# A gated delta-rule layer with expert mixing: a new body of the pass, with masked scaled decays, 32x32 turns and solves in two steps

## What is computed

```python
def step(state, inp):
    q_t, k_t, v_t, g_t, b_t = inp
    state = state * jnp.exp(g_t)[..., None, None]
    kv_mem = jnp.einsum('bhkv,bhk->bhv', state, k_t)
    delta = (v_t - kv_mem) * b_t[..., None]
    state = state + jnp.einsum('bhk,bhv->bhkv', k_t, delta)
    o = jnp.einsum('bhkv,bhk->bhv', state, q_t)
    return (state, o)
```

## Time and profile before

| | us |
|---|---|
| median of three runs | 3445.3 (3440.46 to 3448.35) |
| the profiled execution | 3440.67 |
| its span, first to last instruction | 3438.8 |
| zc of the first pass to zc of the last, 63 passes | 337.2 to 3388.5 |
| mean granted TensorE clock | 0.953 |

### The profile page before, as it was taken

One profiled execution on the slowest core, in us unless ns is written; L12 is line 12 of the kernel. 1 busy time (PEld: TensorE's weight loads), 2 busy tenths in 40 slices (PEclk: granted clock), 3 DMA queues, 4 the chain that ended last, 5 costly groups with the idle time before them and its releaser, 6 DMA issues.

```text
span 3438.8 us, 56504 instructions
## 1 busy us (share of the span) xinstructions
PE 2992.4 (87%) x18444; PEld 2451.1 (71%) x18444; DVE 3012.3 (88%) x9101; ACT 1794.2 (52%) x4111; POOL 2306.0 (67%) x2650
## 2 busy tenths in 40 slices
PE   7844999989998989899989988898989899998997
PEld 4422777778776777677767777777777777777776
DVE  5996999989998999899989898998899898989996
ACT  3322555555554555455545555555555555555553
POOL 0005777777767776777778777877777667877764
PEclk9976999999999999999999999999999999999999
DMA  1003545544555545454545554544555454544553
GB/s 60 1 1 104 137 132 141 135 131 132 137 139 135 131 133 139 130 133 133 141 126 138 134 138 124 149 127 134 138 138 137 125 139 132 146 129 135 144 132 89
DMA packets 541827, 427.98 MB, mean 124 GB/s; under 512 B 247008, under 2 KB 450784, under 8 KB 541536
## 3 DMA queue, kind: packets, MB, share of 16 engines
q1 hardware_dynamic: 476000, 222.98, 24.0%
q0 software_dynamic: 65536, 201.39, 22.0%
HBM read 345.61 MB, written 45.09 MB: 114 GB/s over the span
## 4 chain that ended last, share of the span: by engine, by line
DVE 36%; POOL 35%; PE 14%; issue 9%; DMA 5%; ACT 1%; SPq 0%; DVEq 0%; POOLq 0%; ACTq 0%
POOL rows L952 22%; DVE rows L1193 9%; POOL xg L931 9%; DVE qkv L1177 6%; DVE mix L1210 4%; POOL rms L928 3%; DVE E L1165 3%; DMA rows<-table,pick 3%; PE ps L579 3%; PE ps L500 3%; PE ps L517 2%; PE ps L665 1%; DVE topi L1024 1%; DVE xg L1147 1%; PE ps L521 1%
## 5 line engine op out<-in xcount | busy, mean ns | idle before, releaser
L952 POOL DMA_INDIRECT rows<-table,pick x1024 | 1157.2, 1130 | 326.3 <-issue 326.3
L551 PE MATMUL ps<-X,AT 128*128 128x128 f32 x3072 | 417.7, 294 | 119.2 <-DMA XT<-whole 119.2
L551 PEld LDWEIGHTS ps<-X,AT 128*128 128x128 f32 x3072 | 392.9, 207 | 169.8 <-DMA XT<-whole 167.3
L806 ACT ACTIVATE qkv<-qkv 128x512 f32<-128x512 f32 x256 | 161.5, 631 | 518.6 <-DVE qkv L1177 518.6
L571 PE MATMUL ps<-XT,E 128*128 128x128 f32 x3072 | 400.6, 277 | 0.0
L801 ACT ACTIVATE raw<-ps 128x512 f32<-128x512 f32 x256 | 152.8, 597 | 433.2 <-PE ps L517 433.2
L1210 DVE SCALAR_TENSOR_TENSOR mix<-rows,zc,mix 128x256 f32<-128x256 f32 x896 | 375.1, 476 | 0.0
L571 PEld LDWEIGHTS ps<-XT,E 128*128 128x128 f32 x3072 | 368.9, 192 | 0.0
L939 POOL TENSOR_SCALAR gm<-cst,gn 128x128 f32<-128x128 f32 x512 | 362.9, 723 | 6.7
L1193 DVE CUSTOM_DVE_ANT_0 rows<-rows,h2c 128x128 f32<-128x128 f32 x1024 | 342.9, 399 | 9.2 <-SPq L328 4.7
L931 POOL TENSOR_SCALAR xg<-xg,rms 128x128 f32<-128x128 f32 x520 | 324.9, 637 | 7.0
(11 more groups left out here) (167 smaller groups left out, 6333.4 us busy)
## 6 DMA issues: line engine op xcount, KB each, us to landing
Wvz<-wvz SPq DMA_DIRECT2D x64, 512.0 KB, 3.3
xb<-xnT SPq DMA_DIRECT2D x64, 512.0 KB, 4.4
whole<-AT SPq DMA_DIRECT2D x128, 256.0 KB, 3.6
X<-whole SPq DMA_DIRECT2D x128, 256.0 KB, 3.9
XT<-whole SPq DMA_DIRECT2D x128, 256.0 KB, 4.4
wo<-woh SPq DMA_DIRECT2D x65, 256.0 KB, 4.4
Wkq<-wkq SPq DMA_DIRECT2D x64, 256.0 KB, 2.5
rows<-table,pick POOLq DMA_INDIRECT x1024
```

The source lines that it names most:

```text
L551: done = mm(ps[:, g, (a % 4) * P:(a % 4 + 1) * P], AT_b[:, a, :], src[:, a, :], start=True, stop=True)
L952: pool.indirect_dma_start(rows[:, m, :], None, table[:, :], bass.IndirectOffsetOnAxis(ap=pick[:, m:m + 1], axis=0)).then_inc(gathered, 16)
```

## The change

The same 64 passes and pipelining, with a new body:

- **Masks and decays.** GpSimd makes gm with two `affine_select` (causal, 128x512 each) in place of eight products, and two more selects mask the decays DT after the exponential. ScalarE then scales the decays by head, in place (`scale_decays`, eight operations). With that, AT comes from two VectorE operations, straight from the key products in PSUM, with a factor of -1 and no identity; the elimination adds where it subtracted. MT comes from two VectorE operations, also straight from PSUM. km and kq, and GpSimd's MT products, are gone.
- **Levels.** Two in place of three. The first E is put with `copy_predicated` into E0, which holds the identity. XT comes from TensorE as before, and X from VectorE turning XT's PSUM in blocks of 32x32 (`turn_X`). The second E leaves PSUM as four small rectangles on ScalarE (`take_E`), into E1, which also holds the identity.
- **Solves.** The last level isn't formed. Each solve is done in two steps: XT times RV (`blocks`), ScalarE copies the upper half to Y, TensorE carries it to the lower half (`carried`), VectorE adds it to RV (`lower_rhs`), XT times RV again, ScalarE copies Y. `scaled_y` is gone, and Kd is scaled by kcol.
- **Second output.** Its product with MT moves from the end of the pass to the beginning of the next (`second_output`).
- **Order.** GpSimd's `finish` stands ahead of the picks, so that the sixteen gathers follow each other; the first eight wait for half_v (four mixes of each half done). VectorE's masked E stands ahead of the second outputs; mean_square comes behind key_norms and the fourth mix. On ScalarE squares and the RV copies stand ahead of silu(0).
- xb, a copy of the tokens' columns that SyncE loaded every pass, is gone; the projection reads xnT.

The diff, cut to its core:

```diff
@@ GpSimd @@
+            def causal(dst, src, done):
+
+                pool.affine_select(dst, src, [[0, 4], [1, P]], ALU.is_ge, zero, base=0, channel_multiplier=-1).then_inc(done, 1)
...
-                for a in range(TASKS):
-                    pool.tensor_scalar(gm[:, a, :], mask(C_LE), gn[:, a:a + 1], None, ALU.mult).then_inc(sm["gm_p"], 1)
+                for g in range(2):
+                    causal(gm[:, 4 * g:4 * g + 4, :], gn[:, 4 * g:4 * g + 4].unsqueeze(2).broadcast_to([P, 4, P]), sm["gm_p"])
...
-                pool.wait_ge(sm["diff_t"], at("diff_t", 2))
+                for g in range(2):
+                    pool.wait_ge(sm["exp_done"], at("exp_done", g + 1))
+                    d = DT[:, 4 * g:4 * g + 4, :]
+                    causal(d, d, sm["causal_p"])
                 if f + 1 < PASSES:
                     gate_sums(f + 1, 2 if n is None else 1)
                 if n is not None:
-                    pool.wait_ge(sm["e_v"], at("e_v", 3))
+                    finish()
+                    pool.wait_ge(sm["half_v"], at("half_v", 1))
                 picks(f)
...
                 gather(0)
                 if n is not None:
-                    finish()
                     pool.wait_ge(sm["mix_v"], at("mix_v", 1))
                 gather(K // 2)
...
-                    pool.tensor_tensor(MT2[nx][:, 4 * g:4 * g + 4, :].rearrange("p (t r) i -> p t r i", r=R),
...
@@ TensorE @@
                 if place["u"]:
+                    second_output(MT2[nx])
                     pe.wait_ge(sm["inv_in"], last("inv_in"))
...
+                    for g in range(2):
+                        pe.wait_ge(sm["e_v"], at("e_v", g + 1))
+                        if g == 0:
+                            pe.wait_ge(sm["o1_v"], at("o1_v", 1))
+                        elif place["u"]:
+                            pe.wait_ge(sm["qs_s"], last("qs_s"))
+                        level_X(0, g)
...
@@ ScalarE @@
                 if front:
                     take(0)
                 if back:
-                    take_X(0, 0)
                     take_XT(0, 0)
-                    take_X(0, 1)
-                if front:
-                    silu(0)
-                if back:
                     take_XT(0, 1)
                     act.wait_ge(sm["xg_v"], at("xg_v", 2))
                     squares(1)
...
+                if front:
+                    silu(0)
+                if back:
+                    take_E(0)
+                    take_E(1)
+                if front:
+                    act.wait_ge(sm["s_v"], at("s_v", 1))
+                    act.wait_ge(sm["causal_p"], at("causal_p", 2))
+                    scale_decays(0)
...
@@ VectorE @@
+                def turn_X(g):
+
+                    dve.wait_ge(sm["xt_t"], at("xt_t", g + 1))
+                    V.transpose(X[:, 4 * g:4 * g + 4, :].rearrange("p a i -> p (a i)"), ps[:, 4 + g, :]).then_inc(sm["x_v"], 1)
...
+                def triangle(r):
+
+                    dve.wait_ge(sm["scaled_s"], at("scaled_s", 4 * r + 4))
+                    V.scalar_tensor_tensor(out=of_head(AT, r), in0=keys_by_time(), scalar=-1.0, in1=of_head(DT, r), op0=ALU.mult, op1=ALU.mult)\
+                        .then_inc(sm["at_v"], 1)
...
-                    level(0, 0)
-                    level(0, 1)
                     dve.wait_ge(sm["silu_e"], at("silu_e", 1))
-                    expert_mix(0, 3)
+                    expert_mix(0, 1)
+                    turn_X(0)
+                    turn_X(1)
                 if front:
                     for d in (1, 2, 3):
                         tap(0, d)
                 if back:
+                    expert_mix(1, 3)
+                if front:
+                    key_norms()
+                if back:
                     expert_mix(3, 4)
-                    level(1, 0)
-                    level(1, 1)
-                if front:
-                    strict_part()
-                if back:
                     mean_square()
                 if front:
+                    triangle(0)
+                    triangle(1)
```

375 lines of the change are left out of this document (189 added, 186 removed).

## The result

The changed kernel takes 3771.1 us (median; 3759.6 to 3778.0) beside 3446.8 of the kernel before on the same chip: 1.094 times, 95% interval 1.090 to 1.097. It is slower, as forecast, but by 324 us where 205 were forecast, and outside the range of 3460 to 3740. The profiled execution took 3778.0 us, its span 3776.3.

The account below looks back on a forecast made before the run. Bound: a loop of GpSimd's gathers and scaling in series with VectorE's head and dots. 3.1 + 3.56 + 12.64 + 30.2 = 49.5 us, plus 1.6 for the clock; 3440.7 + 63 x 3.6 - 20 = 3647, say 3650; range 3460 to 3740.

Parts of the forecast that it names:

- VectorE's head, 12.64 + 1.6 for the clock = 14.2: From zc to mean_square landing, which GpSimd's rms awaits: 12.64 us, plus 1.6 for XT products at half clock.
- The rival in which the clock stays up: TensorE's clock doesn't fall behind its pause, so the pass is only 2.0 us longer: 3547 us, chance 19%.
- GpSimd's finish, 6.72: GpSimd's scaling of the output, rms and xg, moved ahead of the pick: still 6.72 us in series.
- Gathers with pick and h2c, 0.59 + 22.92: GpSimd's pick and copy 0.59 us, then sixteen gathers as 10.77 + 0.3 + 11.85, all in series.
- the faster rival: VectorE's two-input operations slow GpSimd's gathers, 2.9 us over plain price; relieved, pass 44.5 to 47.0, 3386 us at 47.0; chance 15%.
- Landing, first dot's start 2.8 after the last gather's end: Gathered rows land 2.8 us after the last gather's end; without MT the first dot ends at 3.1, not 4.81.
- The dots, 3.56 behind the first: VectorE's time from the first dot to zc, taken unchanged at 3.56 us.
- the prediction's third rival: GpSimd's selects hold VectorE's dots as MT did; first dot ends at 5.5, not 3.1: 3801 us, chance 10%.
- The long passes, 20 us less: Seven long passes with gather stalls hold nearly all of 55.6 us excess; stalls cost only 7 x 4.7 = 33: 20 less.
- landing a little worse: Allowance in the range's upper end, 3740, beyond both unknown VectorE forms at 1.05 us (3704).
- beside the path: Work off the loop: VectorE 3.8 us less, ScalarE 2 us more net under its idle, xb's 512 KB load gone.
- a closing through the Y copies: Sign of being wrong: the loop closes through another engine, as by the solves' Y copies on ScalarE.

Follow-up runs that it names:

- m2: Kernel before with 1 MB of extra transfers that SyncE starts 3 to 4 us before a pass's last gather ends: 3680.7 us, 1.054 times the kernel before.
- e4: Changed kernel with SyncE's 1 MB of X16 and XT16 loads held until the gathered rows have landed: 4064.9 us, 1.160 times the kernel before.
- m1: Kernel before with GpSimd's two MT products made twice, first into a tile that nothing reads: 3644.9 us, 1.039 times the kernel before.
- e3: Changed kernel with GpSimd's four selects held until VectorE's dots are done: 4052.2 us, 1.158 times the kernel before.
- c8: c5 with ScalarE's second silu of z ahead of the last silu and GpSimd's selects held until the dots are done: 3385.8 us, 0.971 times the kernel before.
- e9: Changed kernel gathering eight rows a pass in place of sixteen, all other work unchanged: 3509.9 us, 1.006 times the kernel before.
- c5: Changed kernel, fourth mix and mean square before key norms, finish between gather halves, first silu before RV copies, 8 unread matmuls a pass: 3396.5 us, 0.971 times kernel before.
- c9: c5 with added matmuls of 256 columns in place of 512, placed 2, 1, 4, 2: 3387.9 us, 0.972 times the kernel before.

## Why the prediction was right and wrong

The direction and most of the mechanism held: a closed loop of VectorE's head, GpSimd's finish, sixteen gathers, landing and dots. In the first trace its terms add to the pass: 14.0 from zc to rms, 7.5 for rms and xg, 22.9 from there to the last gather's end, 4.2 to the first dot, 5.1 to zc, 53.6 in the mean. Against the prediction's steps:

- **VectorE's head, 12.64 + 1.6 for the clock = 14.2.** Measured 14.0 (14.2 in the middle). In the pass above ss is waited for 2.1 us, as the sum had it, and the first level of XT takes 3.31 us at half clock behind a pause of 3.4 us (5 forecast). The rival in which the clock stays up is out: the clock between 2 and 6 us after zc is 0.63 in the mean.
- **GpSimd's finish, 6.72.** 7.5 measured, +0.7: it now runs beside VectorE's AT products and taps, and eight xg take 5.98 in place of 4.93. The step "that only moves 6.72 us inside the loop" took a duration along to a place with other company.
- **Gathers with pick and h2c, 0.59 + 22.92.** 22.9 measured, -0.6. Of the 2.9 of the faster rival (gathers slowed by VectorE's operations) 0.8 came, a gather taking 1.07 in the mean where it took 1.13; that VectorE's operations are the reason is not shown.
- **Landing, first dot's start 2.8 after the last gather's end: the first step that failed.** 4.2 in the mean, 4.4 in the middle: +1.4 to 1.6. It took the landing from the earlier trace rows as a constant of the gather. That is the landing with the loads behind it; in the changed kernel 1 MB of them starts ahead of the last gather's end (m2, and e4 with the loads held: 2.3).
- **The dots, 3.56 behind the first: the second step that failed.** From the first dot's start 5.1 (5.3 in the middle), where 3.5 is the undisturbed price: +1.2 against the 3.86 that 3.56 and the first dot make. This is the prediction's third rival at a lower price. It had two selects as one hold on the first dot, 2.4 us; in fact each of four selects holds one dot by 0.43 (0.71 less 0.28), 1.7 in all. m1 shows a hold by MT's products too. What spoke against it, dots at 0.28 beside the gm products of the kernel before, is true (515 dots lie wholly inside one such product, at 0.28 in the middle) but was no evidence for a select. That the rival's 3801 lies near the 3778 of the profiled execution is luck: the landing filled what the selects did not cost.
- **The long passes, 20 us less.** All 56 us went: no pass stands out. The terms above come to 2.45 us a pass more than forecast, 154 us, of which this gives 36 back; 12 came in setup and tail.
- **Operations that no row showed.** A select takes 0.63 where 1.3 was taken, a turn and a masked copy 0.72 each where 0.6 was. The selects were off the path except through the dots, and with them shorter and the pass longer GpSimd waits 16 us for the mean square and not about 10. (The sum's "64 products of a task" are those of a pass; its 7.1 us counts them so.)

So 131 us were missed between 3647 and 3778. Landing and dots alone make 2.6 us a pass, 163 us; the other terms take some 30 back. The range failed for the same reason: it held one "landing a little worse" and left the selects out, and the two came together.

A page has a rule on such a hold. The Trainium skill, "SBUF — State Buffer", section "SBUF: two separate sides", says that a VectorE operation with two SBUF inputs and a GpSimd operation that reads SBUF take a shared pair of ports in turn, each for its whole instruction. The rows of the selects agree: a dot beside a select of 0.63 takes 0.71, and in e3 and c8, with no select beside the dots, they take 0.28 in every pass. The gm products of the kernel before, which read SBUF too, do not: a dot inside one takes 0.28. So here the rule holds for some of GpSimd's operations, and the runs don't tell what sets them apart.

What the prediction had no length for is the second loop. It counted TensorE's and ScalarE's work as "beside the path", with a closing through the Y copies only among the signs of being wrong. On the first chip the first loop hid it, being 4 us longer (by e9's length, which is from another chip). The runs put it at 49 us a pass (e9), 47 with the clock up (c5), 46.8 with the filling shorter, when VectorE's taps and ScalarE's series are what is left (c9; the loop through GpSimd, by the working in c9's expectation 44.8 to 46.5, is then close). On the first chip it cost nothing visible; on the others it closed the pass, together with the late results beside the long row of gathers.

Not settled: why TensorE's results come late there and not on the first chip, and what part the recording has in it; why e3 and e4 cost 1.8 and 1.9% more than the changed kernel on such a chip; how much of m2's 184 us is the landing and how much the later blocks. The first silu's move was not run by itself, and no edit was run on the first chip.

## What to carry to other kernels

A loop that closes through one engine can have another close behind it: before pricing a move, follow the chain that leaves the first loop's engines out, and ask what the pass would be if the first were free; halving a load that only the first loop carries shows it in one run. A duration read from a trace belongs to its neighbours: for each term that the change shifts in time, list what will then run beside it (transfers beside a landing, GpSimd beside VectorE's two-input operations) and bound it with a row that has such a neighbour. And where TensorE waits in every pass, filling the pauses with work that nobody reads can pay: here 3.6% for 8 matmuls a pass. A run that misses its number can still hold the proof of a single term in its trace, as e4's did for the landing.
